# Graph attention on one core: two of the four column blocks of wq·wkᵀ from scaled fp16 parts instead of fp32

## The reference

```python
h = maximum(layernorm(x), 0)
v = h @ weight;  q = h @ wq;  k = h @ wk
alpha = maximum(q @ k^T, 0) * (adj != 0)
alpha = softmax(alpha, axis=1)
out = x + alpha @ v
```

## Time and profile before

| | |
|---|---|
| time before, median of 3 runs | 413.31 us (412.66 to 413.48) |
| the profiled execution's own time | 412.91 us |
| its span | 411.1 us |
| PE busy | 405.3 us (99%) |
| DVE, ACT, POOL busy | 298.1, 277.7, 264.7 us |
| granted PE clock | 1.00 of full speed all through |

### The profile page before, as it was taken

How to read it: one execution, slowest core, us unless ns; L and a number is a source line. 1 busy time by engine, 2 the same in 40 slices (tenths; PEclk the granted TensorE clock), 3 DMA queues, 4 the chain that set the end, 5 groups by cost and what they waited for, 6 DMA issues and landing times.

```text
span 411.1 us, 9529 instructions
## 1 busy us (share of the span) xinstructions
PE 405.3 (99%) x3580; PEld 321.7 (78%) x3580; DVE 298.1 (73%) x571; ACT 277.7 (68%) x592; POOL 264.7 (64%) x286
## 2 busy tenths in 40 slices
PE   8999999999999999999999999999999999999995
PEld 5444545979797997979798897979889797979884
DVE  5797789896867676776767777676777667656565
ACT  4749887765867677766777776776867777644534
POOL 0767896979495866759395775939577584910004
PEclk9999999999999999999999999999999999999999
DMA  8973858989889897997969498985978599493022
GB/s 284 373 110 67 217 103 217 232 205 217 181 208 191 245 155 212 189 204 188 192 212 196 156 214 199 197 218 173 198 241 158 156 220 181 75 197 112 2 104 102
DMA packets 161641, 75.03 MB, mean 183 GB/s; under 512 B 135360, under 2 KB 143808, under 8 KB 161600
## 3 DMA queue, kind: packets, MB, share of 16 engines
q1 hardware_dynamic: 161168, 73.81, 77.6%
q10 hardware_dynamic: 432, 0.66, 0.4%
HBM read 24.12 MB, written 16.78 MB: 99 GB/s over the span
## 4 chain that ended last, share of the span: by engine, by line
PE 90%; DVE 4%; DMA 2%; ACT 1%; SPq 1%; issue 1%; POOL 0%; DVEq 0%; POOLq 0%
PE bank L1166 10%; PE bank L1165 10%; PE bank L1163 10%; PE bank L1181 10%; PE bank L1180 10%; PE bank L1178 10%; PE s_bank L1192 3%; PE s_bank L1193 3%; PE s_bank L1194 3%; PE bank L1199 2%; PE bank L1200 2%; PE bank L1201 2%; PE bank L1320 2%; PE bank L1322 2%; PE bank L1321 2%; DMA x_sb<-in_x 2%
## 5 line engine op out<-in xcount | busy, mean ns | idle before, releaser
L423 POOL TENSOR_TENSOR hn_lo<-h,hn_hi 128x512 f16<-128x512 f32 x64 | 74.0, 1166 | 53.1 <-ACT hn_hi L554 52.9
L544 ACT ACTIVATE h<-x_sb,shift,rstd 128x512 f32<-128x512 f32 x64 | 50.0, 804 | 24.0 <-POOL shift L418 23.6
L449 POOL TENSOR_TENSOR hn_lo<-s,hn_hi 128x512 f16<-128x512 f32 x56 | 63.3, 1163 | 0.3 <-ACT hn_hi L559 0.3
L1163 PE MATMUL bank<-hT_hi,mt_hi 128*128 128x256 f16 x224 | 61.1, 273 | 0.0
L1165 PE MATMUL bank<-hT_lo,mt_hi 128*128 128x256 f16 x224 | 61.1, 273 | 0.0
L1180 PE MATMUL bank<-wt_lo,hT_hi 128*128 128x256 f16 x224 | 61.1, 273 | 0.0
L1166 PE MATMUL bank<-hT_hi,mt_lo 128*128 128x256 f16 x224 | 61.1, 273 | 0.0
L1178 PE MATMUL bank<-wt_hi,hT_hi 128*128 128x256 f16 x224 | 61.1, 273 | 0.0
L1181 PE MATMUL bank<-wt_hi,hT_lo 128*128 128x256 f16 x224 | 61.1, 273 | 0.0
L559 ACT ACTIVATE hn_hi<-s 128x512 f16<-128x512 f32 x56 | 33.8, 625 | 25.6 <-POOL s L438 19.9
L1180 PE MATMUL bank<-w_lo,hT_hi 128*128 128x256 f16 x168 | 45.8, 273 | 0.0
(11 more groups left out here) (169 smaller groups left out, 1115.2 us busy)
## 6 DMA issues: line engine op xcount, KB each, us to landing
out_h<-x_sb SPq DMA_DIRECT2D x63, 256.0 KB, 2.1
x_sb<-in_x SPq DMA_DIRECT2D x15, 1024.0 KB, 5.5
adj_sb<-in_adj SPq DMA_DIRECT2D x16, 256.0 KB, 5.3
hn_hi<-in_L_gnn_wq SPq DMA_DIRECT2D x4, 256.0 KB, 5.6
x_sb<-in_x SPq DMA_DIRECT2D x2, 512.0 KB, 7.2
w_sb<-in_L_gnn_weight SPq DMA_DIRECT2D x2, 512.0 KB, 8.7
hn_lo<-in_L_gnn_wk ACTq DMA_DIRECT2D x2, 256.0 KB, 3.8
hn_lo<-in_L_gnn_wk SPq DMA_DIRECT2D x2, 256.0 KB, 3.7
```

The costliest lines, as they stand in the source:

```text
L423: nc.gpsimd.tensor_tensor(hn_lo[:, s, b], h[:, b], hn_hi[:, s, b], ALU.subtract).then_inc(h_split, 1)
L449: nc.gpsimd.tensor_tensor(low, s32[:, f], high, ALU.subtract).then_inc(s_split, 1)
L544: nc.scalar.activation(h[:, b], x_sb[:, s, b], ACT.Relu, bias=shift[:, b:b + 1], scale=rstd[:, b:b + 1]).then_inc(h_made, 1)
L1163: nc.tensor.matmul(o, bh[:, k, cols], ah[:, :, k], start=first and c == 0 and k == 0, stop=False, skip_group_check=True)
```

## The change

Column blocks 0 and 1 of M are still made in fp32. For blocks 2 and 3, wk and the two row blocks of wq are scaled and split into fp16 parts, and each block is made by 12 fp16 matmuls. For this the scales of wk and wq must be known early, so the one chain of the maxima becomes three, each over one weight: `KEY`, then `QUERY`, then `W`. ACT makes the parts `wk_hi` (four) and two fp32 copies `wk_scaled`, from which POOL makes two of the `wk_lo`; DVE makes the other two. `m_scale` becomes a product of the two scales, and blocks 2 and 3 are brought back by a constant, `M_BACK`. V of graphs 0 to 2 is made in an order that follows the arrival of parts (high parts before `w_lo`). POOL makes the four sums of weight without waiting for `w_split`, and group 1's statistics and scales are taken in two halves, around `m_lo`. The last half-graph's output is issued by ACT instead of SP.

```diff
         @block.gpsimd
             pool.wait_ge(consts_made, 5)
-            first_scales(0)
-            first_scales(1)
+            for k in range(2):
+                pool.wait_ge(wk_scaled_made, k + 1)
+                pool.wait_ge(wk_hi_made, k + 1)
+                nc.gpsimd.tensor_tensor(wk_lo[:, k], wk_scaled[:, k], wk_hi[:, k], ALU.subtract).then_inc(wk_lo_pool, 1)
+            first_scales(0, 0)
+            first_scales(0, 1)
             for b in range(GB):
                 lo_of_h(0, 0, b)
-            pool.wait_ge(w_split, K)
+            for k in range(2):
+                pool.wait_ge(w_loaded[k], 16)
 ...
-            layernorm_scales(1)
+            first_scales(1, 0)
+            first_scales(1, 1)
             for b in range(GB):
                 lo_of_h(1, 1, b)
+            layernorm_scales(2)
...
         @block.scalar
-            for r in range(1, K):
-                act.wait_ge(wqT_filled, r + 1)
-                nc.scalar.activation(wqT[:, :, r], wT_bank[r % 2], ACT.Copy).then_inc(wqT_copied, 1)
-            for b in range(GB):
-                normalise_h(0, 0, b)
-                if b > 0:
-                    hi_of_h(0, 0, b - 1)
-            hi_of_h(0, 0, GB - 1)
+            act.wait_ge(wqT_filled, 2)
+            nc.scalar.activation(wqT[:, :, 1], wT_bank[1], ACT.Copy).then_inc(wqT_copied, 1)
+            act.wait_ge(scale_step, KEY_SCALED)
+            act.wait_ge(wkT_copied, K)
+            for k in range(K):
+                if k < 2:
+                    nc.scalar.activation(wk_scaled[:, k], wkT[:, k].rearrange("p r n -> p (r n)"), ACT.Copy,
+                                         scale=key_scale).then_inc(wk_scaled_made, 1)
+                nc.scalar.activation(wk_hi[:, k], wkT[:, k].rearrange("p r n -> p (r n)"), ACT.Copy,
+                                     scale=key_scale).then_inc(wk_hi_made, 1)
+            def hi_of_wq(r):
+                act.wait_ge(wqT_filled, r + 1)
+                act.wait_ge(scale_step, QUERY_SCALED)
+                nc.scalar.activation(wq_hi[:, r - 2], wT_bank[r % 2], ACT.Copy, scale=query_scale).then_inc(wq_hi_made, 1)
+            normalise_h(0, 0, 0)
+            normalise_h(0, 0, 1)
+            hi_of_h(0, 0, 0)
+            hi_of_wq(2)
+            normalise_h(0, 0, 2)
+            hi_of_h(0, 0, 1)
+            hi_of_wq(3)
+            normalise_h(0, 0, 3)
+            hi_of_h(0, 0, 2)
+            hi_of_h(0, 0, 3)
...
         @block.vector
+            for r in range(K):
+                key_max(r)
+            top(KEY)
+            query_max(0)
+            top_row(KEY, 0)
+            query_max(1)
+            power(KEY, 0, 0)
+            query_max(2)
+            stats_first(0)
+            stats_first(1)
+            query_max(3)
+            top(QUERY)
+            stats_first(2)
+            top_row(QUERY, 1)
+            stats_first(3)
+            power(QUERY, 1, KEY_SCALED)
...
+            top(W)
+            lo_of_wq(2)
+            top_row(W, 2)
+            lo_of_wq(3)
+            power(W, 2, M_SCALED + 1)
+            lo_of_wk(2)
+            lo_of_wk(3)
             for k in range(K):
                 vec.wait_ge(w_hi_made, k + 1)
...
         @block.tensor
+            spread_top(QUERY, 1)
+            product_m(1, range(1))
+            spread_row(QUERY, 1)
+            product_m(1, range(1, K))
+            pe.wait_ge(wk_hi_made, K)
+            for c in (2, 3):
+                pe.wait_ge(wq_hi_made, c - 1)
+                for k in range(K):
+                    scaled_m(c, wq_hi, wk_hi, k, start=k == 0)
+            spread_top(W, 2)
+            pe.wait_ge(wk_lo_pool, 2)
+            for c in (2, 3):
+                for k in range(2):
+                    scaled_m(c, wq_hi, wk_lo, k)
+            spread_row(W, 2)
+            for c in (2, 3):
+                pe.wait_ge(wq_lo_made, c - 1)
+                for k in range(K):
+                    scaled_m(c, wq_lo, wk_hi, k)
+            for k in (2, 3):
+                pe.wait_ge(wk_lo_vec, k - 1)
+                for c in (2, 3):
+                    scaled_m(c, wq_hi, wk_lo, k, stop=k == K - 1)
```

More of the change, by code:

```diff
@@ L157, in graph_attention_kernel @@
         shift = sb("shift", [N, GB], F32)
+        W, QUERY, KEY = range(3)
+        w_scale, key_scale, query_scale = (scale_of[:, i:i + 1] for i in (W, KEY, QUERY))
+        m_factor = W_TOP / (4 * D)
+        M_BACK = m_factor / 2.0 ** (2 * W_SHIFT)
         row_max = sb("row_max", [N, GB], F32)
@@ L735, in _ @@
-            act.wait_ge(scale_step, 5)
+                nc.scalar.activation(w_hi[:, k], w_sb[:, k], ACT.Copy, scale=w_scale).then_inc(w_hi_made, 1)
             for k in range(K):
                 act.wait_ge(m_filled, k + 1)
-                nc.scalar.activation(m_hi[:, k], M_BANK[k], ACT.Copy, scale=m_scale[:]).then_inc(m_hi_made, 1)
+                nc.scalar.activation(m_hi[:, k], M_BANK[k], ACT.Copy,
+                                     scale=m_scale[:] if k < 2 else M_BACK).then_inc(m_hi_made, 1)
@@ L1338, in _ @@
             transpose_wq(3)
-            product_m(1)
-            pe.wait_ge(top_step, 1)
-            nc.tensor.transpose(top_bank[0:3, 0:N], w_top[:], ident[:]).then_inc(top_filled, 1)
-            product_m(2, range(1))
-            pe.wait_ge(top_step, 3)
-            pe.wait_ge(consts_made, 5)
-            nc.tensor.matmul(top_bank[:, N:N + 3], ones[:], top_diag[:], start=True, stop=True).then_inc(top_filled, 1)
-            product_m(2, range(1, K))
-            product_m(3)
-            for b in range(GB - 1):
-                pe.wait_ge(hT0_landed[b], 2 * 16)
-                whole_product_v(0, b)
+            spread_top(QUERY, 1)
@@ new lines, in _ @@
+            spread_row(W, 2)
[7 more added lines that the diff above has]
+                    scaled_m(c, wq_hi, wk_lo, k, stop=k == K - 1)
+            pe.wait_ge(hT0_hi_landed[0], 16)
+            for k in range(K):
+                pe.wait_ge(w_hi_made, k + 1)
+                first_v(0, hT_hi, w_hi, k, start=k == 0)
@@ new lines, in _ @@
+            pe.wait_ge(hT0_lo_landed[0], 16)
+            for k in range(K):
+                first_v(0, hT_lo, w_hi, k)
+            pe.wait_ge(hT0_hi_landed[1], 16)
+            for k in range(K):
+                first_v(1, hT_hi, w_hi, k, start=k == 0)
+            for k in range(K):
+                pe.wait_ge(w_split, k + 1)
+                first_v(0, hT_hi, w_lo, k, stop=k == K - 1)
+            for k in range(K):
+                first_v(1, hT_hi, w_lo, k)
+            pe.wait_ge(hT0_lo_landed[1], 16)
@@ L1353, in _ @@
+            for k in range(K):
+                first_v(1, hT_lo, w_hi, k, stop=k == K - 1)
+            pe.wait_ge(hT0_hi_landed[2], 16)
+            for k in range(K):
+                first_v(2, hT_hi, w_hi, k, start=k == 0)
+            for k in range(K):
+                first_v(2, hT_hi, w_lo, k)
+            pe.wait_ge(hT0_lo_landed[2], 16)
+            for k in range(K):
+                first_v(2, hT_lo, w_hi, k, stop=k == K - 1)
             pe.wait_ge(m_split, K)
```

188 lines of the change are left out of this document (112 added, 76 removed).

## The result

The changed kernel takes 418.08 us (median of 4 runs, 417.76 to 418.70), the kernel before 412.99 us (median of 4, 412.62 to 413.48). The ratio is 1.0125 with a 95% interval from 1.0113 to 1.0137: slower by 4.7 to 5.7 us. The profiled execution took 417.76 us, 4.85 more than that of before.

A forecast was written before the change was run, and what follows sets the result against it. PE, busy 405.3 of 411.1 us, was taken as the bound, the end set by when T of group 0 begins. 4.6 (T) + 2.0 (scores) - 0.5 (`p_lo`) - 0.2 (output) = +5.9 on 412.9: 418.8 us, range 416.8 to 420.3.

The forecast's parts named there:

- PE's own sum: PE's matmuls, transposes and products with ones: fp16 blocks save 1.8 us, extra maxima cost 0.8, -1.0 us in all.
- The chain up to the scale of weight: Key scale at 9.4, ACT normalising from 15.08, PE gaps for wq; scale of weight at 22.4 against 18.6 before.
- DVE and POOL in one stretch, the largest term: Behind weight's scale, DVE's `lo_of_wk` and `w_lo` alternate with POOL's sums; last `w_lo` at 31.75 instead of 26.4.
- T of group 0: PE's V and DVE's `m_lo` both end about 36.3, so T begins there, 4.6 us later.
- The scores: PE waits 2.0 us for group 0's fourth `tT_lo`; scores begin at 51.3, +6.6 against 44.70.
- Behind it: After the scores: the wait for `p_lo` goes, -0.5 us; last output issued on ACT, -0.2; exponentials at 56 to 56.5.
- POOL not in the way: Rival, chance 0.10: POOL's sums do not stop DVE, `w_lo` ends at 26.4, T at 31.9; 413 us.
- PE is the only bound: Rival, chance 0.13: PE's sum of -1.0 us counts and V by parts hides the rest; 411.7 us.

The follow-up runs named there:

- e12: Kernel before, M all fp32, with group 1's statistics and scales in halves, `wt_lo` late, group 2's scales before POOL's sums of M: 412.15 us, ratio 0.9987.
- e8: Changed kernel with sums waiting for `w_split`, `wt_lo` late, group 1's scales between the sums and a shorter chain to weight's scale: 412.14 us, ratio 0.9982.
- e1: Changed kernel with the old wait put back: POOL's four sums of weight wait for `w_split`; 414.97 us, ratio 1.0049.
- e2: Kernel before with only POOL's wait for `w_split` replaced by the wait for the load of weight: 414.82 us, ratio 1.0045.
- e3: Changed kernel with DVE's two `wt_lo` moved behind the third and fourth `tT_lo` of group 0: 416.79 us, ratio 1.0094.
- e6: Changed kernel with all four statistics of group 1 taken ahead of `m_lo` again: 417.85 us, ratio 1.0120.
- e11: Changed kernel with the last half-graph's output issued by SP again: 417.88 us, ratio 1.0123.
- e4: Changed kernel with POOL's sums of weight waiting for `w_split` and the two `wt_lo` behind the `tT_lo`: 413.63 us, ratio 1.0019.
- e7: Changed kernel with sums waiting for `w_split`, `wt_lo` late, and POOL making group 1's scales between its sums of weight: 412.88 us, ratio 1.0002.
- e5: Changed kernel with half of group 0's scales before POOL's `wk_lo`, and both high parts of wq made consecutively on ACT: 417.05 us, ratio 1.0102.

## Why the prediction was right, and where its numbers were off

The forecast was 418.8 us with its own range from 416.8 to 420.3; measured were 418.08 by median and 417.76 in the profiled run. Step by step:

- **PE's own sum.** -1.0 was forecast. Busy from 4 us up to T, PE had 27.40 us in the kernel before, 26.56 in e12 (the same matmuls, another start-up), 27.08 in the changed kernel and 25.90 in e8 (the same matmuls as the changed kernel). By the lowest of each the saving is 0.7; with the same matmuls it differs by 1.2 between the changed kernel and e8, so the -1.0 lies inside what they leave open. Over the whole span PE's busy time fell by 0.3 (405.3 to 405.0), where the forecast had some 1. That the saving is worth nothing while the chain is late held.
- **The chain up to the scale of weight.** The forecast was 22.4; the scale's instruction ends at 21.74. The key scale ended at 8.80, not 9.4, and the rest followed: ACT normalised from 14.39 (15.08 forecast), the two gaps of PE for the parts of wq were 0.39 and 0.69 (0.8 and 1.0 forecast). The steps were the right ones, each a little too long.
- **DVE and POOL in one stretch, the largest term.** This is the step that carried the result, and e1 and e2 show it by taking the wait in and out of both kernels: -3.1 and +1.8 us. Its size was over-estimated. I counted 1.25 for POOL and 0.6 for DVE, 1.85 a turn; POOL's sums start 1.67, 1.68 and 1.79 apart. The last `w_lo` ended at 30.29, not 31.75: 0.8 of this came with POOL's last `lo_of_h`, which ended at 22.37 and not at 23.15, and 0.7 is what the turns were shorter. `pow` of weight took 0.15 us at 21.40, inside POOL's `lo_of_h`, and held nothing up. One reading in this step was wrong: the four `m_lo` of before (28.96 to 31.68) did not run beside POOL's sums, the last of which ended at 28.40, but beside its short instructions for group 1's scales. That the sums do not slow `m_lo` came true all the same, as e1's rows show.
- **T of group 0.** 36.3 was forecast, 34.88 measured, +3.15 in place of +4.6: the mis-sized term of the sum. The last `m_lo` ended at 34.45, so V on PE was the later of the two by 0.4, where the forecast had them meet. Behind the last `w_lo` PE had 21 matmuls left (30.34 to 34.88), not 20.
- **The scores.** A wait of 2.0 for the fourth `tT_lo` was forecast, 1.70 measured, with `wt_lo` at 3.24 us (3.25 forecast); e3 showed its place, and e6 that it is a gate of its own. +6.6 was forecast for their start and +5.0 measured; of the 1.6 less, 1.4 come from T and the rest from the wait.
- **Behind it.** The wait of 0.5 for `p_lo` did go, but it was worth 0.2: from scores to first outputs 13.23 us before, 13.04 after. The exponentials began at 54.45, 4.0 later than before, and not at 56 to 56.5. The -0.2 for the last output did not come: in the changed kernel DVE ends at 412.70 and the span 3.2 later; before, at 407.89 and 3.2 later. ACT's issue of the last outputs in the changed kernel:

```profile
412.34 0.87 ACTq L878 DMA_DIRECT2D out_h<-x_sb  x2
```

It ends 0.51 us behind DVE, where SP's ended 0.68 behind it, and yet the span ends no sooner; e11 shows no difference either.

The sum was +5.9 by the forecast and +4.85 by the traces: 3.15 + 1.85 (the scores' further delay) - 0.2 = 4.8.

Of the rivals, the one with POOL not in the way (413) described what e4 and e7 then made by edits: with the wait back and `wt_lo` late, 413.63 and 412.88. The one that PE is the only bound (411.7) wasn't reached even by e8, 412.14. The measured time lies in the forecast's own range and outside all the rivals'. From the changed kernel to e8 the 5.9 us go back in these parts: the wait for `w_split` 3.1, `wt_lo` late 1.3, scales between the sums 0.75 (e4 to e7), the earlier scale of weight 0.7 (e7 to e8).

Left open is what the fp16 parts could give at best. e8's PE is busy 0.66 less than e12's up to T and begins T 0.34 earlier, the first outputs too, and the medians are equal. From the first matmul of M to the first of V, PE takes 15.12 us in e8 (8.16 to 23.28) and 15.50 in e12 (8.11 to 23.61), and from there to T 7.8 in both: in these two traces the fp16 parts shorten M by 0.4, with the idle 0.78 for `lo_of_wk` still in it. No kernel was run without that wait, and none with M in fp32 and V in the order by arrival.

## What to carry to other kernels

A wait that seems to ask for more than the data needs may be what keeps two engines apart: before it goes, lay the instructions of POOL and those of DVE with two inputs in SBUF side by side for that stretch, and count how many of one stand between those of the other. Here each POOL sum in between made DVE's chain 1.0 us longer (1.68 for a turn against 0.68 for a `w_lo` alone). Work saved on the busiest engine is worth only what the next gates (T, the fourth `tT_lo`, `p_lo`) let through, so follow the change to the point where both kernels run alike, here the first outputs, and read the gain there. And when a rearrangement around a new idea gains, try it on the kernel without the idea: here it gave all of the gain that the runs can tell apart.

## What the runs showed of the hardware that I had not expected

- The alternation of DVE and POOL is cheaper than the sum of both: with nothing beside them, POOL's sums start 1.23 us apart and `w_lo` 0.68 apart (2.73 for four) in e1, 1.91 together, but a turn of both takes 1.68 us (the starts of POOL's sums in the changed kernel). About 0.2 us of a turn overlaps.
- Engines do not meet only at semaphores, as the opening of this document has it: POOL's sums and the two-input instructions of DVE held each other up inside their durations. DVE's statistics, with one input, did not: BN_STATS took 0.66 to 0.68 us beside POOL's sums of weight in the kernel before, and 0.66 to 0.69 with POOL idle.
- Small instructions on DVE are not alike. On one column, `pow`, TENSOR_SCALAR on int32 with one input, took 0.15 us beside a running POOL instruction, and `m_scale`, SCALAR_TENSOR_TENSOR with two inputs from SBUF, took 1.07 and 1.08 us in e8 and e5, where a `wk_lo` of POOL runs beside it, and 0.16 in the changed kernel, where it does not. On three columns TENSOR_SCALAR waited as well: `pow` had taken 0.56, and `ipow` took 1.23 in e2, beside POOL's last sum, where it took 0.15 in the kernel before with POOL idle. From e2:

```profile
26.20 1.23 DVE L1040 TENSOR_SCALAR ipow<-pow 128x3 int32<-128x3 int32 x1
```

So both the form of the instruction and its columns went with the wait; no run was made to find where the line lies.
